# Row scores of the first batch issued beside the weights' setup, and the last half finished on VectorE

## The reference

```python
xn = _layernorm(x)
s = _L0_attn_ref(xn, ...)      # softmax(q (Wa k)^T) (v Wb^T), 1024 x 1024 scores, one head
g = _silu(_L0_ffn_ref(xn, ...))  # silu/gelu MLP 128-512-512-512-128, ternary weights times scales
x = x + s * g
xn = _layernorm(x)
s = _L1_attn_ref(xn, ...)      # 8 heads: gated recurrence over the rows, output product Wo + bo, layer norm
g = _silu(_L1_ffn_ref(xn, ...))  # 16-head attention plus top-2 of 8 experts
x = x + s * g
```

## Time and profile before

| | |
|---|---|
| median of 3 runs | 1064.15 us (1063.66 to 1066.93) |
| the profiled execution's own time | 1064.29 us |
| its span in the trace | 1062.5 us |
| mean granted TensorE clock | 0.979 of full |
| PE busy | 980.8 us (92%) |
| DVE busy | 568.7 us (54%) |
| ACT busy | 757.9 us (71%) |
| POOL busy | 203.9 us (19%) |

### The profile page before, as it was taken

One profiled execution on the slowest core, in us unless ns is written; L12 is line 12 of the kernel. 1 busy time (PEld: TensorE's weight loads), 2 busy tenths in 40 slices (PEclk: granted clock), 3 DMA queues, 4 the chain that ended last, 5 costly groups with the idle time before them and its releaser, 6 DMA issues.

```text
span 1062.5 us, 16258 instructions
## 1 busy us (share of the span) xinstructions
PE 980.8 (92%) x6122; PEld 548.3 (52%) x6122; DVE 568.7 (54%) x1377; ACT 757.9 (71%) x922; POOL 203.9 (19%) x144
## 2 busy tenths in 40 slices
PE   2699899999999989999989989999998998999995
PEld 1588743344378853334347875334436886333431
DVE  6845744554465663472654574456447357346352
ACT  5253589988853479997955357998894436999885
POOL 3200021322120020240230002043022001114123
PEclk9799999999999989999999998999999999999998
DMA  6000033000000013200000002300000000320000
GB/s 236 1 2 1 1 49 62 1 2 1 1 22 2 1 19 50 43 2 2 1 20 2 1 1 39 51 22 1 1 1 21 2 1 10 50 33 1 1 1 23
DMA packets 14428, 20.66 MB, mean 19 GB/s; under 512 B 2848, under 2 KB 11136, under 8 KB 14080
## 3 DMA queue, kind: packets, MB, share of 16 engines
q1 hardware_dynamic: 14336, 19.41, 8.5%
HBM read 7.85 MB, written 2.10 MB: 9 GB/s over the span
## 4 chain that ended last, share of the span: by engine, by line
PE 72%; DVE 9%; ACT 6%; issue 6%; SPq 4%; POOL 2%; DMA 1%; DVEq 0%; POOLq 0%; ACTq 0%
PE ps L1090 69%; SPq L351 4%; ACT big L1046 3%; PE ps L1489 1%; DVE st L275 1%; DVE mx L483 1%; POOL st L866 1%; DVE xn L451 1%; DVE wk L731 1%; DVE wk L541 1%; ACT xn L1018 1%; DVE flags L419 1%; DVE wk L476 1%; PE ps L1110 1%; DVE qk_max L556 0%
## 5 line engine op out<-in xcount | busy, mean ns | idle before, releaser
L1046 ACT ACTIVATE big<-ps 128x1024 f32<-128x1024 f32 x512 | 493.8, 1034 | 50.5 <-PE ps L1090 48.6
L1090 PE MATMUL ps<-big,vaug 128*32 128x512 f32 x2048 | 272.6, 604 | 3.7 <-DVE wk L731 2.5
L1090 PE MATMUL ps<-hid 32*128 32x512 f32 x1024 | 130.5, 493 | 3.5 <-ACT big L1046 1.9
L1090 PE MATMUL ps<-hid,fw_sb 128*128 128x512 f32 x416 | 100.6, 396 | 0.0
L866 POOL TENSOR_TENSOR st<-st 128x4 f32<-128x4 f32 x16 | 16.2, 1011 | 433.9 <-DVE st L530 325.8
L965 ACT ACTIVATE wk<-ps,cols_sb 128x512 f32<-128x512 f32 x64 | 40.5, 687 | 78.3 <-PE ps L1090 74.2
L1090 PEld LDWEIGHTS ps<-hid 32*128 32x128 f32 x1024 | 49.1, 181 | 77.1 <-issue 42.0
L1090 PEld LDWEIGHTS ps<-hid,fw_sb 128*128 128x128 f32 x416 | 77.8, 188 | 17.6
L879 POOL TENSOR_TENSOR qz<-qz,wk 128x512 f32<-128x512 f32 x32 | 41.2, 1287 | 232.6 <-DVE wk L701 232.6
L1090 PEld LDWEIGHTS ps<-big,vaug 128*32 128x32 f32 x2048 | 41.0, 108 | 69.7 <-issue 41.6
L719 DVE SCALAR_TENSOR_TENSOR big<-ps,sm,big 128x128 f32<-128x128 f32 x128 | 44.2, 346 | 46.6 <-PE ps L1090 35.9
(11 more groups left out here) (210 smaller groups left out, 1630.5 us busy)
## 6 DMA issues: line engine op xcount, KB each, us to landing
hid<-spl SPq DMA_DIRECT2D x288, 32.0 KB
xnext<-in_x SPq DMA_DIRECT2D x4, 512.0 KB, 3.9
out<-qz SPq DMA_DIRECT2D x8, 256.0 KB, 2.3
big<-in_fw SPq DMA_DIRECT2D x1, 1877.0 KB, 9.2
wk<-in_lw SPq DMA_DIRECT2D x1, 1476.0 KB, 14.3
big<-in_fw SPq DMA_DIRECT2D x1, 939.0 KB, 11.0
cst_sb<-in_cst SPq DMA_DIRECT2D x1, 440.0 KB, 4.5
xn<-in_aw SPq DMA_DIRECT2D x1, 320.0 KB, 5.2
```

The lines of the kernel that those rows point to most:

```text
L1046: up(ms_exp, a.activation(prob[:, at:at + 2 * CH].rearrange("p (h n) -> p h n", n=CH), ps[:, bank:bank + 2, :], ACT.Exp, scale=HDM ** -0.5))
L1090: return t_.matmul(out_, lhsT, rhs, start=start, stop=stop, **kw)
```

## The change

The first batch's row scores 0 and 1 and their maxima are issued before the flag is made, not after.

- ScalarE: after xT it copies the small part of `fw`, the two halves of r, the large part of `fw`, then `lw`. It waits for the flag only ahead of the first silu.
- GpSimd: its difference of the small part waits for the first of the two `fw` copies, not the second.
- VectorE: after the small tables come the low parts of r and the halving of Wo, then row maxima 0 and 1 of batch 0. Then `weight_flags()`: difference of the large part (which waits for both copies), the two absolute maxima, the larger of both, the `iflag`, the bias row. Then maxima 2 to 7. The wait for `lw_ok` comes behind the maxima.
- TensorE: row scores 0 and 1 and u of tile 0 follow the r products. The sum of the flags, the sums for the bias row, a small product that waits for `iflag`, and the branch register come after u of tile 5, ahead of row scores 4. They use banks 0 and 1, and there is one flag product instead of two.
- End of the last batch: half 1's addition of `moe`, product and addition of `xres` are on VectorE, with semaphores `sg_last` and `fin_last`; GpSimd does half 0 alone. SyncE's last store waits for `fin_last`.

```diff
@@ -230,7 +230,7 @@
-        sg_ok = sig("sg_ok", 2)
+        sg_ok, sg_last, fin_last = sig("sg_ok", 2, 0, 1), sem("sg_last"), sem("fin_last")
         scan_ok, qs_ok, o_ok, sum_ok = sig("scan_ok", 8), sig("qs_ok", 8), sig("o_ok", 2), [sig("sum_ok0"), sig("sum_ok1")]
@@ -256,7 +256,7 @@
         ex_mm, ex_ok, msum_ok = sig("ex_mm", 2 * NT), sig("ex_ok", 2 * NT), sig("msum_ok", 1, 1)
-        g2_ok, fin_ok = sig("g2_ok", 2), sig("fin_ok", 2, 1)
+        g2_ok, fin_ok = sig("g2_ok", 2), sig("fin_ok", 2, 1, 1)
         stored = sig("stored", 32, 1)
@@ -354,7 +354,10 @@
                 for c in range(NCH):
-                    sp.wait_ge(fin_ok.sem, fin_ok.at(b, c + 1))
+                    if b == B - 1 and c:
+                        sp.wait_ge(fin_last, 1)
+                    else:
+                        sp.wait_ge(fin_ok.sem, fin_ok.at(b, c + 1))
                     o = out[bass.ds(b, 1)].rearrange("o (t p) d -> p (o t) d", p=P)
@@ -408,30 +411,32 @@
             done(v.tensor_tensor(decay[:, 2 * KM:3 * KM], decay[:, KM:2 * KM], cols_sb[:, COL["bv"]:COL["bv"] + KM], ALU.mult))
-            for i in range(2):
-                h_ = FW_HALVES[i]
-                if i == 0:
-                    v.wait_ge(fw_hi_ok, 1)
-                    done(v.tensor_tensor(bigf[:, h_], bigf[:, h_], fw_sb[:, h_].bitcast(F32), ALU.subtract))
-                    so_far()
-                else:
-                    v.wait_ge(fw_dif, 1)
-                done(v.tensor_reduce(flags[:, 4 + i:5 + i], bigf[:, h_], AX.X, ALU.max, apply_absolute_value=True))
             for c in range(NCH):
...
                                 ALU.subtract).then_inc(r_lo.sem, 1)
-            so_far()
-            done(v.tensor_tensor(flags[:, 0:1], flags[:, 4:5], flags[:, 5:6], ALU.max), "flags")
-            v.wait_ge(setup_p, 3)
-            v.tensor_scalar(iflag[:, 0:1], ps[:, 2, 0:1], 0.0, None, ALU.is_gt).then_inc(wide_ok, 1)
-            v.wait_ge(wide_ok, 1)
             v.wait_ge(wo_in, 16)
             done(v.tensor_scalar(wo_sb[:, :], wo_sb[:, :], 0.5, None, ALU.mult), "half Wo")
-            v.wait_ge(setup_p, 4)
-            done(v.tensor_tensor(rows_sb[:, 0:D], rows_sb[:, 0:D], ps[:, 0, 0:D], ALU.add))
-            so_far()
-            v.wait_ge(lw_ok, 1)
+            def weight_flags():
+                for i in range(2):
+                    h_ = FW_HALVES[i]
+                    if i == 0:
+                        v.wait_ge(fw_hi_ok, 2)
+                        done(v.tensor_tensor(bigf[:, h_], bigf[:, h_], fw_sb[:, h_].bitcast(F32), ALU.subtract))
+                        so_far()
+                    else:
+                        v.wait_ge(fw_dif, 1)
+                    done(v.tensor_reduce(flags[:, 4 + i:5 + i], bigf[:, h_], AX.X, ALU.max, apply_absolute_value=True))
+                so_far()
+                done(v.tensor_tensor(flags[:, 0:1], flags[:, 4:5], flags[:, 5:6], ALU.max), "flags")
+                v.wait_ge(setup_p, 3)
+                v.tensor_scalar(iflag[:, 0:1], ps[:, 0, 0:1], 0.0, None, ALU.is_gt).then_inc(wide_ok, 1)
+                v.wait_ge(setup_p, 4)
+                done(v.tensor_tensor(rows_sb[:, 0:D], rows_sb[:, 0:D], ps[:, 1, 0:D], ALU.add))
+                v.wait_ge(wide_ok, 1)
+                so_far()
@@ -484,6 +489,10 @@
                     row_maximum(t)
+                    if b == 0 and t == 1:
+                        weight_flags()
+                if b == 0:
+                    v.wait_ge(lw_ok, 1)
                 step(v.memset(uaug[:, :, D:D + 1], 1.0))
@@ -823,6 +832,15 @@
+            tl = slice(TPC, NT)
+            v.wait_ge(msum_ok.sem, msum_ok.at(B - 1, 1))
+            v.wait_ge(att_ok.sem, att_ok.at(B - 1, 2 * NG))
+            up(sum_ok[1], v.tensor_tensor(att[:, tl, :], att[:, tl, :], moe[:, tl, :], ALU.add))
+            v.wait_ge(o_done.sem, o_done.at(B - 1, 1))
+            v.wait_ge(g2_ok.sem, g2_ok.at(B - 1, 2))
+            v.tensor_tensor(g2[:, tl, :], g2[:, tl, :], xnv[:, tl, :], ALU.mult).then_inc(sg_last, 1)
+            v.wait_ge(sg_last, 1)
+            v.tensor_tensor(fin[:, tl, :], g2[:, tl, :], xres[:, tl, :], ALU.add).then_inc(fin_last, 1)
             v.br("v_end")
@@ -855,7 +873,7 @@
             bigf, h_ = big[:, :, :, :].rearrange("p a g n -> p (a g n)"), FW_HALVES[1]
-            g_.wait_ge(fw_hi_ok, 2)
+            g_.wait_ge(fw_hi_ok, 1)
             g_.tensor_tensor(bigf[:, h_], bigf[:, h_], fw_sb[:, h_].bitcast(F32), ALU.subtract).then_inc(fw_dif, 1)
@@ -895,12 +913,12 @@
                 g_.wait_ge(msum_ok.sem, msum_ok.at(b, 1))
-                for c in range(NCH):
+                for c in range(NCH if b < B - 1 else 1):
                     tl = slice(c * TPC, (c + 1) * TPC)
...
                 g_.wait_ge(o_done.sem, o_done.at(b, 1))
-                for c in range(NCH):
+                for c in range(NCH if b < B - 1 else 1):
                     tl = slice(c * TPC, (c + 1) * TPC)
@@ -928,16 +946,16 @@
             bigf = big[:, :, :, :].rearrange("p a g n -> p (a g n)")
-            for i in range(2):
-                a.wait_ge(fw_in[i], 16)
-                a.activation(fw_sb[:, FW_HALVES[i]], bigf[:, FW_HALVES[i]], ACT.Copy).then_inc(fw_hi_ok, 1)
-            a.wait_ge(lw_in, 16)
-            a.activation(lw_hi[:, :], wk[:, 0:NLW], ACT.Copy).then_inc(lw_hi_ok, 1)
+            a.wait_ge(fw_in[1], 16)
+            a.activation(fw_sb[:, FW_HALVES[1]], bigf[:, FW_HALVES[1]], ACT.Copy).then_inc(fw_hi_ok, 1)
             for c in range(NCH):
...
                 a.activation(spl[:, 0, c * CH:(c + 1) * CH], ps[:, c, :], ACT.Copy).then_inc(r_hi.sem, 1)
+            a.wait_ge(fw_in[0], 16)
+            a.activation(fw_sb[:, FW_HALVES[0]], bigf[:, FW_HALVES[0]], ACT.Copy).then_inc(fw_hi_ok, 1)
+            a.wait_ge(lw_in, 16)
+            a.activation(lw_hi[:, :], wk[:, 0:NLW], ACT.Copy).then_inc(lw_hi_ok, 1)
             a.wait_ge(lw_ok, 1)
-            a.wait_ge(wide_ok, 1)
             for b in range(B):
@@ -969,6 +987,8 @@
                 a.wait_ge(msum_ok.sem, msum_ok.at(b, 0))
+                if b == 0:
+                    a.wait_ge(wide_ok, 1)
                 silu_units(0)
@@ -1126,16 +1146,6 @@
                 split3(ps[:, c, :], gh_hi[:, 0:D], gh_lo[:, 0:D], xt_hi[:, sl], xt_lo[:, sl]).then_inc(r_mm.sem, 1)
-            t_.wait_ge(setup_v, marks["flags"])
-            mm(ps[:, 2, 0:1], ones, flags[:, 0:1], True, True).then_inc(setup_p, 1)
-            t_.wait_ge(wide_ok, 1)
-            mm(ps[:, 3, 0:1], ones, flags[:, 0:1], True, True)
-            t_.wait_ge(setup_v, marks["half Wo"])
-            for m in range(KM):
-                ins = mm(ps[:, 0, 0:D], ones, wo_sb[:, m * D:(m + 1) * D], m == 0, m == KM - 1)
-            ins.then_inc(setup_p, 1)
-            wide = t_.value_load(iflag[0:1, 0:1], min_val=0, max_val=1)
             attended = ExitStack()
@@ -1165,6 +1175,16 @@
                         up(u_mm, ins)
+                    if b == 0 and t == TPC + 1:
+                        t_.wait_ge(setup_v, marks["flags"])
+                        mm(ps[:, 0, 0:1], ones, flags[:, 0:1], True, True).then_inc(setup_p, 1)
+                        t_.wait_ge(setup_v, marks["half Wo"])
+                        for m in range(KM):
+                            ins = mm(ps[:, 1, 0:D], ones, wo_sb[:, m * D:(m + 1) * D], m == 0, m == KM - 1)
+                        ins.then_inc(setup_p, 1)
+                        t_.wait_ge(wide_ok, 1)
+                        mm(ps[:, 0, 0:1], ones, ones[:, 0:1], True, True)
+                        wide = t_.value_load(iflag[0:1, 0:1], min_val=0, max_val=1)
                     if t % 2 == 1:
```

## The result

The changed kernel took 1072.22 us in the median of its runs (1068.54 the lowest) against 1064.86 of the kernel before: a ratio of 1.0064, interval 1.0043 to 1.0085. It is slower, by 6.8 us, where 1066.5 us, 2.4 us more than before, was forecast, and the time lies above the range given. Measured twice more beside the kernel before, the same kernel gave 1.0020 (1.0001 to 1.0040) and 1.0056 (1.0029 to 1.0083); the three average 1.0047, 5.0 us. The kernel before against itself gave 1.0023 (0.9999 to 1.0047), so single comparisons here scatter by about 0.2%: the 1.0020 alone would show nothing, the other two are more than twice that. One of the six executions (1125.97 us) and one of a later run with unread products (1349.05 us) ran at a much lower mean granted clock (0.853 and 0.661) and are in no ratio.

What follows compares the result with a forecast made beforehand. TensorE's matmul schedule bounds the steady part, VectorE a 14 us stretch of the start. 1064.29 plus 5.0 (later start) less 2.6 (earlier end) is 1066.7; with the median 0.14 lower, 1066.5 us, range 1058.3 to 1068.4.

Steps and rivals of the forecast that it cites:

- The meetings: Start: VectorE and GpSimd, both with SBUF operands, hold each other off, VectorE until 21.0, then from 25.3 until 31.1.
- L410 at 0.16 us: Start: VectorE's tiny `decay` product was forecast held, about 3.7 us long; unheld at 0.16 would mean the prediction was wrong.
- row for a held scalar operation: Near 252.75 us before: two 128x128 SBUF scalar operations, 0.34 us on average, marked 0.94 beside GpSimd's memset.
- The step that failed: First batch, behind the flags: TensorE regains full clock by about 47, so the last row maximum ends at 52.0.
- the start: First batch through its last row maximum: comes out 4.4 to 6.1 us later, taken as 5.0.
- The half-clock rival: First batch's scores 4 to 7, or later: TensorE at half clock adds 1.7 to 3 us, 1068.3; chance 0.15.
- The end: Last batch: second half's operations on VectorE finish 2.4 to 3.1 us earlier, taken as 2.6.
- the tie: Last batch: VectorE's and GpSimd's additions ready at 1053.31 and 1053.29; GpSimd first gains 2.4 us, VectorE first 3.1.
- The whole sum: Whole kernel: 5.0 us later at its beginning less 2.6 at its close, giving 1066.5 us.
- The sign: Whole kernel, direction of the change: faster 0.29, same 0.53, slower 0.18; 1061.0 to 1067.3 counts as the same.
- The no-holding rival: Whole kernel: VectorE and GpSimd never delay each other, first maxima 3 to 4 us sooner, 1058 us; chance 0.13.
- The rival in which VectorE wins: Start: VectorE's large difference precedes GpSimd's, maxima end at 44.4 to 46.0, about 1060 us; chance 0.22.

Runs made afterwards that it cites:

- unread products: Extra 512-column TensorE products before the flag, results never read: 48 added to the changed kernel, 1.0054 of before; 28 added to a version with both engines' holdings removed, 0.9963.
- the end alone: Kernel before with only the last batch's second half moved to VectorE, its start unchanged: 0.9966 of before.
- the flag by a reduction: Kernel before with one instruction exchanged, the larger of two flags taken by a two-column reduction instead of a two-input maximum: 0.9974 of before.
- second meeting taken away: Changed kernel, but GpSimd's 2952-column layer-weight difference waits for VectorE's 3754-column difference: 0.9983 of before.

## Why the prediction was wrong, point by point

- **The meetings, right.** Both were placed and priced from the rows before: small difference on GpSimd 16.95 to 21.0 (measured 16.97 to 21.15), VectorE at its difference at 25.3 behind GpSimd at 24.7 (25.30 and 24.64), flags at 41.5 (41.32), row update at 44.4 (44.21). The held operation was the cast three places ahead of L410 (L405 before, L408 after), not L410, which took 0.17 us. L410 at 0.16 us stands in the prediction as a sign of being wrong; the sign came and the sum held, because the cast was held for the same stretch. By the Trainium skill ("SBUF — State Buffer", Who interferes with whom), a cast can enter a two-port mode and then contends with GpSimd for the whole instruction; the 4.19 us agree, where the same cast took 0.22 before. The prediction's own row for a held scalar operation was weak: the two at 252.75 are of the form `xn<-xn`, which averages 0.45 us, not of the one that averages 0.34. What shows it is the halving of Wo, 2.38 and 2.82 us instead of 0.43.
- **The step that failed:** "The maxima end between 51.4 and 53.1; I take 52.0, since the clock came back 5.7 us after work resumed and would be back by about 47." It came back 7.9 and 11.0 us after work resumed. Nor did the upper end hold: half clock over all the scores was priced at 1.7 us of waits, and maxima 4 to 7 waited 3.1 us in the first trace, 1.6 in the second and 3.0 in the third. From the flags to the last maximum 10.5 us were forecast; 13.3, 11.9 and 13.3 were measured. The 5.7 us were carried over from a stretch in which TensorE had the products of scores 0 and 1 queued behind the flag and kept ahead of VectorE. In the changed kernel scores 0 to 3 are issued before the flag, so behind it TensorE waits 1.48 us for maximum 2 and is busy 6.12 of 7.60 us. (For the same reason it is idle from 29.1, not from about 24, and for 12.2 us.) The traces of all runs agree: full speed came back 5.7 to 6.4 us after work resumed in the four traces with the products queued behind the flag (the kernel before twice, the end alone, the flag by a reduction, there counted from Wo's products), and 7.7 to 11.0 us after it in the eight with the wait for maximum 2 and no unread products. That the thinner stream is the reason is argued from this; no run changes it alone. The maxima ended at 53.0 to 54.6, the start cost 6.0 to 7.7 us instead of 5.0. The half-clock rival, given 0.15, is what happened; its 1068.3 fits the first trace (1068.5) and was 2.4 us short of the third (span 1068.9, with the 1.8 us around it 1070.7). Its own price, up to 3 us on top of the forecast, reached 1069.5, but the range stopped at 1068.4.
- **The end, right:** GpSimd won the tie by 0.03 us, 2.4 us (2.6 taken).
- **What was not in the sum:** stretches at half clock in the later batches, which the kernel before has as well, 2.4 us in one batch between two executions of one kernel. With the start's they make the spans of the changed kernel 2.8 to 6.4 us over before; the first measurement, 6.8 us, lies just above that, and its own interval begins at 4.6. I gave the range half clock in one place only and no width for this.
- **The whole sum.** Forecast 2.4; the start cost 2.7 more, the end gave 0.2 less, the later batches gave 1.0 back: 4.3, the profiled execution. The other 2.5 us of the 6.8 lie between that execution and the rest and stay open.
- **The sign** was right, though the prediction gave slower only 0.18 and the same 0.53: later start, earlier end, more of the former. The no-holding rival, 0.13, is excluded. The rival in which VectorE wins was excluded for this kernel and real for one that differs by a wait: 46.5 measured where 44.4 to 46.0 was worked out, again by the half clock.

Open is why the median of timed executions lies 0.6 to 5 us above the profiled ones (span plus 1.8 us), and whether the half-clock stretches alone make it; no trace of such an execution was at hand. Their mean granted clock does not tell: 0.979 at 1068.54 us, 0.987 at 1071.8, 0.981 at 1076.15.

## What to carry to other kernels

Before moving work of VectorE or GpSimd, write down the times at which both want operands in SBUF and who is first: here one wait of 0.64 us on the idle engine was worth 6.5 to 8.2 us of the start, more than the whole reordering cost. Taking one held operation away handed most of the stall to the next that could be held; order the two engines with a semaphore, or choose reductions or PSUM operands, which ran beside GpSimd at their usual length, for what must overlap. Work issued early from TensorE's queue leaves a hole where it stood: ask at which clock TensorE comes back from its next gap, and whether it then waits. Read that clock from the spacing of equal products as well as from the granted clock.

## What the runs showed of the hardware

- A 128x1 operation with two SBUF inputs took 3.13 us beside GpSimd, a 128x2 reduction 0.14 us at the same place; a 128x512 tensor_scalar in SBUF was held as well (2.38 and 2.82 us instead of 0.43).
- GpSimd's operation is marked from when it asks: 10.13 us for 6.45 us of work, 6.38 for 4.2. VectorE's is too: 9.71 us for 4.06.
- A 128x128 cast in SBUF was held as well (4.19 us instead of 0.22), a 128x512 subtraction with one input in PSUM was not (0.69 us at 18.67 beside GpSimd).
- Behind 6.4 to 14.9 us of idle TensorE, products ran at the spacing of half clock, from where work resumed, for 5.7 to 6.4 us with the queue full (four traces) and for 7.7 to 11.0 us with a wait of 1.5 us in the stream (eight traces).
- The granted clock read 1.00 over such a stretch in two traces (second meeting taken away; the kernel before again) and 0.50 in the other ten: products of 512 columns 0.43 us apart show half clock where it does not.
- Unread products ahead of the flag moved the half clock to 46.7 to 49.9 and, in that trace, to 73.9 to 77.3; it did not shorten the run.
